# A fused expert, attention, expert block: GpSimd normalises half of the second layer's tokens early, and unread products and weight splits move

## The chip, the cores and the metric

The kernel runs on one core of a Trainium2 chip. The metric is the device time of one execution in microseconds; of the kernel before, three timed runs are given and their median is the time to be beaten. An expert stage, an attention stage and a second expert stage run one after the other in a single launch.

## What is computed

The input x has 8 sequences of 256 tokens with 256 features. The reference does three residual steps:

```python
x = x + 0.5 * ffn(layernorm(x), router_w, w1, v1, w2)   # "layer 0" of the kernel
x = x + attn(layernorm(x), Wq, bq, Wk, bk, Wv, bv, Wo, bo)
x = x + 0.5 * ffn(layernorm(x), router_w, w1, v1, w2)   # "layer 1" of the kernel
```

The expert step routes each of the 2048 tokens to 8 of 64 experts by the softmax of the router's logits, normalises the 8 weights, keeps the first 32 tokens of each expert, and computes `(silu(x w1) * (x v1)) w2` for these 64 x 32 slots, which are added back to their tokens by weight. Attention has 16 query heads and 4 key/value heads of 128, all in float32 accuracy.

## The kernel before, in words

**Tiling.** x stays on chip as 16 tiles of 128 tokens (`x`, 128 x 16 x 256). Experts are taken in 16 groups of 4, so that 4 experts x 32 slots fill 128 partitions. Attention runs in 4 blocks of 512 tokens with 16 steps each (2 heads of one sequence by a step).

**An expert stage** (`expert_layer` on each engine). TensorE transposes the tokens and makes the logits; VectorE finds the top 8 (`masks`, L875) and the keys of the first 32 tokens of each expert (L900 to L932, ending in `slot_token` and `slot_index`). Meanwhile ScalarE normalises the tokens into `xn` (`normalise`, L606), GpSimd makes the weights `expw` (L506 to L528), and SyncE writes both to `token_table` in HBM (`store_table`, L405). When `slot_index` is ready and all table writes have landed (`table_written`, L531), GpSimd gathers the slots, one indirect DMA for each group (L538), five in flight.

**The expert steps** (`slot_step`, 17 of them, s = 0 to 16). In step s TensorE transposes the slots of group s + 1 (L1179), adds up the results of group s - 3 (`sum_slots`: L1191 in layer 1 only, L1207), transposes the hidden values of group s - 1 (L1242), multiplies group s up (L1249) and group s - 1 down (L1259). ScalarE copies the transposed slots (L564) and hidden values (L568), makes the gate (L574) and the high half of y (L578); VectorE the weight of the slots (L851 to L855), the one-hot marks (L858), `hidden` (L864) and the low half of y (L871). A chain of dependences runs through a step: up, gate, hidden, transpose, copy, down. All queues are in order.

**Unread products.** `keep_busy` (L1211) multiplies `router_w` by `ident` into a bank that nobody reads. It stands where TensorE has nothing to do: 16 products before step 0, 20 after layer 0's steps, 12 more in layer 1's routing, 4 after the first transposes of attention.

**Splits.** The attention weights come as float32 and are split into two float32r parts: `split_high(n)` on ScalarE (L677), then `split_low(n)` on VectorE (L998). They go by number: 0 and 1 are Wk, 2 and 3 the first part of Wq, 4 and 5 Wv, 6 and 7 the next part of Wq, 8 and 9 Wo, 10 and 11 Wq, and so on. Splits 0 and 1 are done in the last two steps of layer 0, 2 to 5 after them; the others between the first 9 projections of attention (`first_fills`) and the steps of its first block.

**Order of loads.** SyncE's queue loads the experts' weights into places that are reused; layer 1's groups 0 to 6 are loaded from step 12 of the last attention block on (L446 to L449), groups 7 and 8 after the wait for `attention_done`, and behind them come layer 1's stores to the table. GpSimd's own queue waits for `attention_done` before it begins layer 1 (L546).

**Layer norms.** `moment_steps` (L802) makes mean and 1/std on VectorE in short linked instructions. For layer 1 those of tiles 0 to 11 are made in steps 11 and 12 of the last block; `shifts(0, 12)` (L1153), which frees ScalarE to normalise them, comes after its last step.

## Time and profile before

| | us |
|---|---|
| median of 3 timed runs | 658.8 (658.24 to 660.04) |
| the profiled execution | 656.91 |
| its span in the profile | 655.1 |
| layer 0, until the last sum of its steps | 0 to 84.4 |
| attention | about 85 to 567 |
| layer 1's routing, to `slot_index` | about 566 to 590.3 |
| layer 1's steps and output | 594.5 to 655.1 |

| engine | busy us | share of the span |
|---|---|---|
| PE (TensorE) | 617.7 | 94% |
| DVE (VectorE) | 502.9 | 77% |
| ACT (ScalarE) | 386.3 | 59% |
| POOL (GpSimd) | 52.0 | 8% |

How to read it: busy time is a mean over stages with different limits, and a busy PE isn't one at its peak. What a change in one stage is worth is read from that stage, from what its waits ended on. Rows of the timeline give start (us from the start of the span), duration (us), engine, line, operation, tiles, shapes and count, and in brackets the idle time of the engine before it and who ended it.

### The profile page before, as it was taken

Reading aid. Unit: us, or ns where it says so; the run is one execution under the profiler, and the core shown is the slowest. Engines: PE = TensorE matmul, PEld = TensorE weight load, DVE = VectorE, ACT = ScalarE, POOL = GpSimd, SP = SyncE. Lnnn points to the kernel's source line nnn. Section 1 sums busy time; section 2 is a strip of 40 time slices with the busy share of each in tenths; the row PEclk is TensorE's granted clock in tenths of the full one; section 3 lists DMA queues with packets and bytes.
Section 4 is the critical chain, followed back from the end, with each engine's and each line's share of the span. In section 5 each row is a group of like instructions: output and inputs, shape, how many; then the busy total and the mean of one; then the engine's idle time right before and its main releaser. Section 6 shows DMA issues by size and latency. Waiting matters only on the chain.

```text
span 655.1 us, 12187 instructions
## 1 busy us (share of the span) xinstructions
PE 617.7 (94%) x4572; PEld 533.3 (81%) x4572; DVE 502.9 (77%) x1316; ACT 386.3 (59%) x1048; POOL 52.0 (8%) x75
## 2 busy tenths in 40 slices
PE   7489989999999999999999999999999998987995
PEld 5367677999889989999889999989899997764774
DVE  6746668889988778889777788877788888693663
ACT  5734476677666655666665666656566665581442
POOL 3443000000000000000000000000000000034310
PEclk9699999999999999999999999999999999987999
DMA  8999760000000000000000000000000009476781
GB/s 315 352 417 420 295 257 1 2 1 1 1 2 1 1 2 1 1 1 2 1 2 1 2 0 1 2 2 1 1 1 2 1 11 419 172 265 220 293 310 43
DMA packets 27621, 62.53 MB, mean 95 GB/s; under 512 B 7014, under 2 KB 17382, under 8 KB 27558
## 3 DMA queue, kind: packets, MB, share of 16 engines
q1 hardware_dynamic: 25398, 55.97, 22.7%
q0 software_dynamic: 1664, 5.30, 2.2%
q8 instruction: 39, 0.64, 0.4%
q10 hardware_dynamic: 496, 0.43, 0.3%
q14 instruction: 24, 0.20, 0.1%
HBM read 54.34 MB, written 7.34 MB: 94 GB/s over the span
## 4 chain that ended last, share of the span: by engine, by line
PE 78%; DVE 10%; DMA 6%; ACT 2%; issue 1%; another core or an unknown queue 1%; POOL 0%; SPq 0%; POOLq 0%; DVEq 0%
PE bank L1407 20%; PE bank L1409 19%; PE bank L1408 19%; PE bank L1463 8%; PE bank L1207 4%; PE bank L1249 3%; DMA slots<-token_table,slot_index 2%; DMA wo_raw<-wo_in 2%; PE bank L1259 2%; PE bank L1179 1%; DVE probsT_lo L1107 1%; DMA x<-x_in 1%; DVE negmax L1072 1%; DVE ln L812 1%; DVE struck L891 1%
## 5 line engine op out<-in xcount | busy, mean ns | idle before, releaser
L724 ACT ACTIVATE probs<-bank,negmax 128x256 f32<-128x256 f32 x256 | 121.4, 494 | 0.7 <-DVE negmax L1072 0.6
L732 ACT CAST probsT_hi<-bank 128x512 fp32r<-128x512 f32 x128 | 68.7, 590 | 71.0 <-PE bank L1463 71.0
L707 ACT ACTIVATE o_hi<-bank,bv 128x512 fp32r<-128x512 f32 x64 | 44.2, 690 | 66.7 <-PE bank L1409 66.7
L1107 DVE TENSOR_TENSOR probsT_lo<-bank,probsT_hi 128x512 fp32r<-128x512 f32 x128 | 81.9, 681 | 0.5 <-ACT probsT_hi L732 0.5
L1072 DVE TENSOR_REDUCE negmax<-bank 128x2 f32<-128x512 f32 x128 | 81.8, 680 | 0.0
L1080 DVE TENSOR_SCALAR probs<-probs,rowinv 128x256 f32<-128x256 f32 x256 | 73.1, 349 | 2.3
L1407 PE MATMUL bank<-wo_hi,o_hi 128*128 128x256 f32 x256 | 73.1, 285 | 0.0
L1409 PE MATMUL bank<-wo_hi,o_lo 128*128 128x256 f32 x256 | 72.6, 284 | 0.0
L1408 PE MATMUL bank<-wo_lo,o_hi 128*128 128x256 f32 x256 | 72.3, 282 | 0.0
L1058 DVE SCALAR_TENSOR_TENSOR o_lo<-bank,bv,o_hi 128x512 fp32r<-128x512 f32 x64 | 48.0, 750 | 28.6 <-ACT o_hi L707 28.4
L1463 PE MATMUL bank<-ident,probs 128*128 128x128 f32 x512 | 66.4, 273 | 0.7 <-DVE probs L1080 0.7
L1463 PEld LDWEIGHTS bank<-ident,probs 128*128 128x128 f32 x512 | 57.3, 140 | 1.1 <-DVE probs L1080 1.1
L724 ACT ACTIVATION_READ_ACCUMULATOR probs<-bank,negmax 128x1 f32 x256 | 57.7, 226 | 0.0
L1407 PE MATMUL bank<-xT_hi,wq_hi 128*128 128x512 f32 x128 | 54.4, 425 | 1.0 <-DVE k_even_lo L1058 1.0
L1407 PE MATMUL bank<-probsT_hi,v_hi 128*128 128x512 f32 x128 | 51.1, 399 | 3.1 <-DVE probsT_lo L1107 2.9
L1409 PE MATMUL bank<-xT_hi,wq_lo 128*128 128x512 f32 x128 | 50.4, 394 | 0.0
L1408 PEld LDWEIGHTS bank<-wo_lo,o_hi 128*128 128x128 f32 x256 | 48.3, 189 | 2.5
L1407 PEld LDWEIGHTS bank<-wo_hi,o_hi 128*128 128x128 f32 x256 | 48.4, 189 | 2.3
L1408 PE MATMUL bank<-probsT_lo,v_hi 128*128 128x512 f32 x128 | 50.1, 392 | 0.0
L1408 PE MATMUL bank<-xT_lo,wq_hi 128*128 128x512 f32 x128 | 50.1, 392 | 0.0
L1409 PE MATMUL bank<-probsT_hi,v_lo 128*128 128x512 f32 x128 | 50.0, 391 | 0.0
L1409 PEld LDWEIGHTS bank<-wo_hi,o_lo 128*128 128x128 f32 x256 | 48.4, 189 | 0.0
(191 smaller groups left out, 1393.2 us busy)
## 6 DMA issues: line engine op xcount, KB each, us to landing
up_r_<-up_in SPq DMA_DIRECT2D x16, 768.0 KB
down_r_<-down_in SPq DMA_DIRECT2D x14, 512.0 KB
up_q<-up_in SPq DMA_DIRECT2D x8, 768.0 KB, 8.7
up_o<-up_in SPq DMA_DIRECT2D x6, 768.0 KB
down_q<-down_in SPq DMA_DIRECT2D x8, 512.0 KB, 9.4
token_table<-xn SPq DMA_DIRECT2D x16, 256.0 KB, 2.4
down_o<-down_in SPq DMA_DIRECT2D x6, 512.0 KB
x<-x_in SPq DMA_DIRECT2D x4, 512.0 KB, 5.6
```

What stands on the lines that cost most here:

```text
L707: nc.scalar.activation(dst, src, ACT.Identity, bias=bias).then_inc(work_high, 1)
L724: nc.scalar.activation(probs[:, n % 2, t, :], scores_ps[head][:, qt * S:qt * S + S], ACT.Exp, bias=negmax[:, n % 2, t:t + 1], accum_out=ro ...
L732: nc.scalar.copy(probsT[0][:, head].rearrange("p c s -> p (c s)"), probsT_ps[head][:]).then_inc(probsT_high, 1)
L1058: nc.vector.scalar_tensor_tensor(lo, src, bias, hi.bitcast(f32), ALU.add, ALU.subtract).then_inc(work_taken, 1)
L1072: nc.vector.reduce_max(negmax[:, n % 2, 2 * head:2 * head + 2], scores_ps[head][:].rearrange("p (t s) -> p t s", t=2), AX.X, negate=True). ...
L1080: last = nc.vector.tensor_scalar(probs[:, n % 2, t, :], probs[:, n % 2, t, :], rowinv[:, n % 2, t:t + 1], None, ALU.mult)
L1107: nc.vector.tensor_tensor(probsT[1][:, head].rearrange("p c s -> p (c s)"), probsT_ps[head][:], probsT[0][:, head].rearrange("p c s -> p ( ...
L1207: last = mm(banks[n][:, D * pair:D * pair + D], marks[:, c:c + P], parts, start=start and pair == 0, stop=stop, skip_group_check=True)
L1407: mm(dst, w[0], m[0], start=start, stop=False, skip_group_check=shared)
L1408: mm(dst, w[0], m[1], start=False, stop=False, skip_group_check=shared)
L1409: return mm(dst, w[1], m[0], start=False, stop=stop, skip_group_check=shared)
L1463: last = nc.tensor.transpose(probsT_ps[head][:, c * S + qt * P:c * S + qt * P + P], probs[:, n % 2, 2 * head + qt, c * P:c * P + P], ident[:])
```

## The change

1. **GpSimd normalises tiles 0 to 7 of layer 1** into a new buffer `early_xn`, which lies where `wv` was, as soon as `moments_ready` reaches 2; `shifts(0, 12)` moves from behind the last step to the end of step 12 of the last block. SyncE writes these rows to the table behind the loads of groups 0 to 6, ahead of its wait for `attention_done`. ScalarE normalises only tiles 8 to 15 in layer 1, 8 to 11 ahead of the two exponentials, 12 to 15 behind them, and the order of stores follows that.
2. **Unread products**: 4 at the head of step 0, 3 in step 1, 4 in step 2 of both layers (those of step 2 into bank 4, behind a wait for `limit_ready`); 14 instead of 20 after layer 0's steps.
3. **Step 16**: of the sums of group 13 only bank 6's stay ahead of the hidden transpose; bank 7's come behind it.
4. **Splits**: `split_high(0)` moves from the end of step 15 to step 16 behind the hidden copy, `split_high(1)` behind y; `split_low(1)` behind the steps; `split_high` 6 to 10 come after projections 1 to 5, 11 after the last one (before: 6 and 7 ahead of all, 8 to 11 after projections 1 to 4).

```diff
         wk = [sb(ctx, f"wk_{n}", [P, KD, KV * DH], f32r) for n in ("hi", "lo")]
+        with ExitStack() as lent:
+            early_xn = sb(lent, "early_xn", [P, TILES // 2, D])
         wv = [sb(ctx, f"wv_{n}", [P, KD, KV * DH], f32r) for n in ("hi", "lo")]
...
+            def store_early_tokens(n):
+                sp.wait_ge(early_ready, 4 * n + 4)
+                store_rows(n, early_xn)
...
             def store_table(layer):
-                store_tokens(0)
                 if layer == 0:
+                    store_tokens(0)
                     store_tokens(1)
-                store_weights(0)
+                    store_weights(0)
+                store_tokens(2)
                 if layer == 1:
-                    store_tokens(1)
-                    store_weights(1)
-                store_tokens(2)
-                if layer == 0:
-                    store_weights(1)
+                    store_weights(0)
+                store_weights(1)
                 store_tokens(3)
...
             for g in range(len(homes_q) + 3):
                 load(1, g)
+            for n in range(2):
+                store_early_tokens(n)
             sp.wait_ge(attention_done, 1)
...
             expert_layer(0)
+            pool.wait_ge(moments_ready, 2)
+            for a in range(TILES // 2):
+                nc.gpsimd.tensor_scalar(early_xn[:, a, :], x[:, a, :], mean[:, a:a + 1], rstd[:, a:a + 1],
+                                        ALU.subtract, ALU.mult).then_inc(early_ready, 1)
             pool.wait_ge(attention_done, 1)
...
                 if layer == 0 and s == GROUPS:
-                    split_high(1)
+                    split_high(0)
...
-                if layer == 0 and s == GROUPS - 1:
-                    split_high(0)
+                if layer == 0 and s == GROUPS:
+                    split_high(1)
...
-                stops = ((8, 8), (4, 6))[layer]
-                normalise(0, stops[0])
+                middle = (TILES // 2, TILES - 4)[layer]
+                normalise(TILES // 2 * layer, middle)
                 for h in range(2):
                     act.wait_ge(scaled_ready, 2 * layer + h + 1)
                     nc.scalar.activation(expw[:, 8 * h:8 * h + 8, :], expw[:, 8 * h:8 * h + 8, :], ACT.Exp).then_inc(exps, 1)
-                    if h == 0:
-                        normalise(*stops)
                 act.wait_ge(moments_ready, 2 * layer + 1)
-                normalise(stops[1], TILES)
+                normalise(middle, TILES)
...
-            for n in range(6, 8):
-                split_high(n)
             act.wait_ge(bq_scaled, 1)
             for n, job in enumerate(first_fills):
                 take_fill(*job)
-                if 1 <= n < 5:
-                    split_high(n + 7)
+                if 1 <= n < 6:
+                    split_high(n + 5)
+                if n == len(first_fills) - 1:
+                    split_high(11)
...
                 if layer == 0 and s == GROUPS:
                     split_low(0)
-                    split_low(1)
...
                 if layer == 0:
+                    split_low(1)
                     split_low(2)
...
+                if last and n == 12:
+                    shifts(0, TILES - 4)
...
-            shifts(0, TILES - 4)
             for t in range(2):
                 spread_of(BLOCKS - 1, t)
...
+                if s == 0:
+                    keep_busy(4)
                 if s < GROUPS:
                     pe.wait_ge(slotsT_ready, sT_seen.add())
                 if s + 1 < GROUPS:
                     transpose_slots(s + 1, (s + 1) % RING)
-                if s >= 3:
+                if s == GROUPS:
+                    sum_slots(layer, s - 3, [0])
+                elif s >= 3:
                     sum_slots(layer, s - 3)
+                elif s == 2:
+                    pe.wait_ge(limit_ready, layer + 1)
+                    keep_busy(4, bank[4])
+                elif s == 1:
+                    keep_busy(3)
                 if s > 0:
                     pe.wait_ge(hidden_ready, hidden_seen.add())
                     nc.tensor.transpose(bank[2][0:F, 0:P], hidden[:],
                                         ident[:]).then_inc(hiddenT_raw, 1)
+                if s == GROUPS:
+                    sum_slots(layer, s - 3, [1])
...
                 if layer == 0:
-                    keep_busy(20)
+                    keep_busy(14)
```

## Rows read from the trace of the kernel before

**Rows 1.** The page: the chain that ended last, by engine.
```profile
PE 78%; DVE 10%; DMA 6%; ACT 2%; issue 1%; another core or an unknown queue 1%; POOL 0%; SPq 0%; POOLq 0%; DVEq 0%
```
**Rows 2.** The chain in order of time (start, us, what), around layer 1's step 0.
```profile
596.62 3.31 another core or an unknown queue
```
**Rows 3.** Windows: us, busy PE, PEld, DVE, ACT, POOL, then PEclk, DMA share, GB/s.
```profile
593.70:600.50 6.80, 2.26 (x24) 1.10 (x23) 1.51 (x7) 1.26 (x4) 3.89 (x5) 0.85 0.50 138
600.50:605.50 5.00, 4.95 (x48) 2.54 (x52) 3.18 (x14) 1.52 (x5) 0.95 (x1) 0.52 1.02 408
```
**Rows 4.** Timeline, layer 0's steps 1 and 5: when hidden was ready, what TensorE waited for.
```profile
40.78 0.25 DVE L864 TENSOR_TENSOR hidden<-gate,bank 128x96 f32<-128x96 f32 x1 [2.02 <-ACT gate L574]
...
41.20 0.27 PE L1242 MATMUL bank<-ident,hidden 128*96 128x128 f32 x1
...
50.16 0.41 PE L1179 MATMUL bank<-ident,slots 128*128 128x128 f32 x2 [0.27 <-DMA slots<-token_table,slot_index]
```
**Rows 5.** Timeline, layer 0's step 16, TensorE and ScalarE.
```profile
80.10 0.27 PE L1242 MATMUL bank<-ident,hidden 128*96 128x128 f32 x1
80.50 0.63 ACT L681 ACTIVATE wk_hi<-wk_raw 128x512 fp32r<-128x512 f32 x1 [0.75 <-DMA wk_raw<-wk_in]
81.03 0.24 ACT L568 COPY hiddenT<-bank 96x128 f32<-96x128 f32 x1
...
81.33 0.64 PE L1259 MATMUL bank<-down_r_,hiddenT 96*32 96x256 f32 x8 [0.96 <-ACT hiddenT L568]
```
**Rows 6.** Timeline, from the last sums of layer 0 to attention's first operand.
```profile
84.26 4.62 PE L1215 MATMUL bank<-router_w,ident 128*128 128x128 f32 x40
...
87.38 1.38 DVE L1046 TENSOR_SCALAR xn<-x,ln 128x256 f32<-128x256 f32 x4
...
89.19 1.13 ACT L681 ACTIVATE wq_hi<-wq_raw 128x512 fp32r<-128x512 f32 x2
...
90.54 1.07 ACT L705 CAST xT_hi<-bank 128x512 fp32r<-128x512 f32 x2 [0.22 <-PE bank L1430]
```
**Rows 7.** Timeline of ScalarE, the first projections.
```profile
93.92 0.63 ACT L681 ACTIVATE wo_hi<-wo_raw 128x512 fp32r<-128x512 f32 x1 [2.30 <-DMA wo_raw<-wo_in]
```
**Rows 8.** Timeline, the end of layer 1's routing: stores, indices, first gather.
```profile
586.34 2.58 SPq L396 DMA_DIRECT2D token_table<-xn  x4
...
590.11 0.17 DVE L932 TENSOR_SCALAR slot_index<-bank 128x16 uint32<-128x16 f32 x1
...
591.52 0.99 POOL L538 DMA_INDIRECT slots<-token_table,slot_index  x1 [7.11 <-issue]
```
**Rows 9.** Timeline of layer 0: the first gather behind its index (ready at 31.57).
```profile
31.87 1.07 POOL L538 DMA_INDIRECT slots<-token_table,slot_index  x1 [6.72 <-DVE slot_index L932]
```
**Rows 10.** Timeline of TensorE, layer 1: the up products of step 1 and of step 3.
```profile
600.93 1.51 PE L1249 MATMUL bank<-up_q,slotsT 128*32 128x192 f32 x16
...
607.52 0.86 PE L1249 MATMUL bank<-up_q,slotsT 128*32 128x192 f32 x16
```
**Rows 11.** Timeline, layer 1's step 16: hidden, and the down products.
```profile
643.11 0.26 DVE L864 TENSOR_TENSOR hidden<-gate,bank 128x96 f32<-128x96 f32 x1 [0.27 <-ACT gate L574]
...
644.99 0.64 PE L1259 MATMUL bank<-down_r_,hiddenT 96*32 96x256 f32 x8 [0.35 <-ACT hiddenT L568]
```
**Rows 12.** The chain in order of time, steps 12 and 14 of the last block.
```profile
550.52 0.17 DVE ln L812
...
559.85 1.15 DVE probs L1080 x4
```
**Rows 13.** Timeline, step 13 of the last block.
```profile
553.56 1.14 DVE L1080 TENSOR_SCALAR probs<-probs,rowinv 128x256 f32<-128x256 f32 x4
...
556.07 1.04 PE L1463 MATMUL bank<-ident,probs 128*128 128x128 f32 x8
```
**Rows 14.** Timeline of GpSimd in layer 1: a one-input copy, and two two-input products.
```profile
570.71 0.40 POOL L511 CAST key_of_group<-key_i 128x256 f32<-128x256 int32 x1
...
581.85 2.56 POOL L527 TENSOR_TENSOR expw<-expw,chosen 128x512 f32<-128x512 f32 x2
```

More of the change, by code:

```diff
@@ L233, in macaron_kernel @@
         xn_ready = sem("xn_ready")
+        early_ready = sem("early_ready")
         xnT_raw = sem("xnT_raw")
@@ L391, in _, with store_rows @@
             rows_of_table = table[0:T, :].rearrange("(h p b) e -> h p b e", h=2, p=P)
+            def store_rows(n, rows):
+                for half in range(2):
+                    sp.dma_start(rows_of_table[half, :, 2 * n:2 * n + 2, 0:D],
+                                 rows[:, 4 * n + half:4 * n + half + 3:2, :]).then_inc(table_written, 16)
             def store_tokens(n):
                 sp.wait_ge(xn_ready, xn_seen.add(4))
-                for half in range(2):
-                    sp.dma_start(rows_of_table[half, :, 2 * n:2 * n + 2, 0:D],
-                                 xn[:, 4 * n + half:4 * n + half + 3:2, :]).then_inc(table_written, 16)
+                store_rows(n, xn)
+            def store_early_tokens(n):
+                sp.wait_ge(early_ready, 4 * n + 4)
+                store_rows(n, early_xn)
             def store_weights(m):
@@ L1181, in transpose_slots, with sum_slots @@
                 last.then_inc(slotsT_raw, 1)
-            def sum_slots(layer, s):
+            def sum_slots(layer, s, banks=range(2)):
                 pe.wait_ge(marked, GROUPS * layer + s + 1)
@@ L1188, in sum_slots @@
                 marks = onehot[:, s % MARKS, :]
-                if layer == 1:
+                if layer == 1 and 0 in banks:
                     for low in range(2):
@@ L1194, in sum_slots @@
                         last.then_inc(bank_summed, 1)
-                for n in range(2):
+                for n in banks:
                     for low in range(2):
@@ L1199, in sum_slots @@
                         last.then_inc(bank_summed, 1)
-                if not final:
+                if not final and 1 in banks:
                     last.then_inc(summed, 1)
@@ L1209, in sum_wide, with keep_busy @@
                 return last
-            def keep_busy(count):
+            def keep_busy(count, unread=bank[3]):
                 for _ in range(count):
-                    mm(bank[3][:, 0:KD * E], ident[:], router_w[:].rearrange("p k e -> p (k e)"),
+                    mm(unread[:, 0:KD * E], ident[:], router_w[:].rearrange("p k e -> p (k e)"),
                        start=True, stop=True)
```

## The prediction

> **What bounds the kernel now.** I read the page first: the chain that ended last is TensorE for 78% and VectorE for 10% [rows 1]. In the 460 us of attention it is TensorE's queue almost throughout; the change touches that stretch only at its two ends, so it can gain or lose only there and in the two expert stages. So the second view is the chain in order of time at these places, and the third the timeline there. They show six spots. (1) In layer 0's first steps TensorE follows a dependence: hidden is ready at 41.03 and its transpose starts at 41.20 [rows 4]. (2) In step 16 of layer 0 ScalarE makes a split of Wk at 80.50, so the hidden copy comes at 81.03 though the transpose began at 80.10, and the down products start at 81.33 [rows 5]. (3) At the start of attention TensorE is held by 20 unread products and ScalarE by two splits of Wq, until xT at 90.54 [rows 6]; then ScalarE, whose queue has a split of Wo next, waits 2.30 us for the load of Wo that lands at 93.9 [rows 7], while a finished k product sits in its bank. (4) Layer 1's indices are ready at 590.28, but the first gather starts at 591.52, because the last four stores to the table were issued from 586.34 to 588.92 [rows 8]. (5) Right behind it the chain has 3.31 us of "another core or an unknown queue" on ScalarE ahead of its first gate [rows 2], and TensorE, busy 2.26 of 6.80 us, falls to a granted clock of 0.52, its lower level, for the next 5 us [rows 3]. (6) In layer 1's step 16 hidden is ready at 643.37 and the down products start at 644.99 [rows 11], eight to ten sums in between.
>
> **The change part by part.** The sum is made against the profiled execution, 656.91 us with a span of 655.1; the median of the runs shown is 658.8, 1.9 above it, and I carry differences over.
>
> *Unread products in layer 0.* One product costs 4.62 / 20 = 0.23 us at full clock [rows 6]. The four of step 0 fall into a wait for the second gather and cost nothing. The three of step 1 and four of step 2 stand ahead of a hidden transpose whose operand is ready by then (0.17 us earlier in step 1 [rows 4]), so all of them go onto the path: 7 x 0.23 = 1.6. Step 5 waited 0.27 us for its gather [rows 4]; that wait goes. Together +1.3 (bounds 0, if the waits on ScalarE's copies swallow more than I see, and +1.6). Their added wait for `limit_ready` is idle: VectorE makes it at 41.4, ahead of step 2. The weights' loads aren't late through this, they are a backlog of the DMA queues until 76 us.
>
> *Step 16 of layer 0.* From the start of the transpose to down 80.10 to 81.33 = 1.23 us. Without the split in front the copy of 0.24 follows the transpose of 0.27, so down comes about 0.6 after it: -0.6. And the transpose itself no longer waits for all eight sums (1.2 us as a group), but for four: -0.6. So -1.2, and the last sum ends about where it did, at 84.4 + 0.1.
>
> *From there to xT.* `split_low(1)` now stands with `split_low(2)` ahead of the layer norm's statistics: one VectorE split of 0.69 less what was waiting, +0.45 on the tokens' normalisation, which ends at 88.76 [rows 6], so 89.2. TensorE has 6 x 0.23 = 1.4 us less in front of the token transposes, so it is waiting for the tokens rather than the other way. ScalarE's two splits of 1.13 us [rows 6] are out of the way. xT comes at about 89.65 instead of 90.54: -0.9.
>
> *The wait for Wo.* The k product then ends near 92.7 and ScalarE, with Wq's split next instead of Wo's, takes it at once: k at 92.7 instead of 94.45, -1.8 in all. Wo's first split now comes after the third projection behind xT, at about 94.5, when Wo (93.9, not moved) has landed. The splits of 0.6 each that are pushed back, 10 and 11, land on ScalarE when it waits for TensorE anyhow, but 11 stands ahead of the first copies of step 0; I give 0.3 for it. **Attention starts 1.5 us earlier** (bounds -2.0, everything kept, and -0.3, if the 0.9 at xT fails and the splits take back the rest).
>
> *The last block.* `shifts(0, 12)` goes from an idle place into step 12, where the chain goes through the linked layer-norm instructions: the last before the maxima is 0.17 us [rows 12], so one more is +0.2. GpSimd starts its eight instructions then, at 550.9. No row shows its tensor_scalar; a one-input copy of 256 elements takes 0.40, and a two-input product of 512 elements 2.56 / 2 = 1.28 [rows 14]. I take 0.5, nearer to the copy, as there is one tensor input: 8 x 0.5 = 4 us, ended at 555. The four stores (1 MB) go into a SyncE queue that then waits until 570, behind seven groups' loads. Cost 0 (bounds: -0.1; the upper one is the rival below).
>
> *Layer 1's table.* ScalarE's eight instructions and four of eight token stores leave. The last store is issued at about 586.4 instead of 588.9; by the 2.6 us that lay between the last issue and the gather [rows 8] it is free at 589.0, ahead of the indices at 590.28. In layer 0 the gather starts 0.3 us behind its index [rows 9]; so 590.56, 0.96 earlier. But the 16 unread products end at 593.7, and the four new ones of step 0 delay the second transposes a little: I count -0.6 (bounds -0.9 and 0).
>
> *Layer 1's first steps.* If the 3.31 us on ScalarE stay, the three products of step 1 lie under them; the four of step 2 cost +0.9. In return TensorE is busy some 1.6 us more before 599, and I take it that the clock stays at its upper level. The price of the lower one: the up products took 1.51 instead of 0.86 [rows 10], and the whole of steps 1 and 2 about 5.3 us against 3.3 in layer 0: -2.0 (bounds -2.3; and +0.5, if the clock falls all the same and the four products cost 0.36 each).
>
> *Layer 1's step 16.* Down 1.6 us behind hidden [rows 11]; with four sums behind the transpose it is 0.5 less. -0.5 (bounds -0.6 and -0.2).
>
> **Sum:** +1.3 - 1.2 for layer 0, -1.6 for the rest up to attention's first steps (together -1.5), +0.2, -0.6, +0.9 - 2.0, -0.5 = **-3.5**, so 653.4 against 656.9 profiled, and 658.8 - 3.5 = **655.3** for the median.
>
> **The rivals.** (A) *ScalarE's 3.3 us go away.* Its queue is 8 instructions shorter there, and at 596.7 an instruction packet crosses the DMA engines, just as the wait begins; in all other steps none such is seen. If it hangs on the place in the instruction stream, it may vanish: step 1 then waits for the third gather and its products, so another 1.6 us: -5.1, 653.7. Against it: other such packets stall nobody. By the Trainium skill (Runtime: NRT & Kernel Launch, Instruction fetch mechanics) an engine fetches the next block of instructions while it executes the present one, mostly hidden; that would speak for another cause, and this trace doesn't settle it. (B) *The clock falls all the same, or the wait moves into a later step.* Then the first steps are +0.5 instead of -1.1, in all -1.9: 656.9. (C) *Slower: GpSimd blocks VectorE in the last block.* In step 13 four probability scalings of 1.14 us run at 553.56, with 1.4 us of slack to the transpose at 556.07 [rows 13]; those at 559.85 are on the chain [rows 12]. If each of them waited for one GpSimd instruction of 1.28 us, the first four cost 5.1 - 1.4 = 3.7 and the next, as GpSimd isn't done by then, some 2.5: -3.5 + 6.2 = +2.7, 661.5. It decides from about 1.0 us an instruction; at 0.5 the slack takes nearly all. For it: nothing else in the trace of attention runs on GpSimd, so it is untried there. Against it: GpSimd's products in the routing run beside VectorE's work whose durations don't change. The Trainium skill has a rule that speaks against the change here (SBUF — State Buffer, Who interferes with whom): VectorE's tensor_scalar in its two-port mode and GpSimd share a port pair, and the later one blocks fully until the first is done. By it each of the first four would wait for up to one instruction, which at 0.5 us is 2.0 less the slack, +0.6 on the sum. No row of before shows such a pair. (D) *The start of attention gives nothing*, as VectorE's splits, which are as many as before, set its pace: -3.5 + 1.8 = -1.7, 657.1.
>
> **How the numbers follow.** Forecast 0.40, A 0.22, B 0.18, C 0.07, D 0.13. The measurement can tell about 0.3%, 2.0 us, from no change. Faster by more than that: the forecast, A, and a third of B and D (by their bounds), 0.72; within: 0.22; slower: 0.06. The forecast's own bounds of the front (-0.3 to -2.0) give 654.8 to 656.5; A reaches below it to 652.9, B and D above it to 658.2. The range is 652.8 to 658.2; left out are C and the corners.
>
> **What would show it.** Steps 1 to 3 of layer 0 later by 0.7 and 1.6 us, its last sum at 84.4 +- 0.3; xT below 90; no wait of ScalarE for Wo, and the first scores 1.5 us earlier; GpSimd's eight instructions from 551 on and their duration, VectorE's scalings beside them still 1.14 for four; first gather of layer 1 0.3 us behind `slot_index`; PEclk 1.00 from 593 on; and the 3.3 us on ScalarE in the same place or not. The forecast is wrong if the clock falls there, if GpSimd's instructions take over 1 us, or if attention's first steps don't keep the lead.

## The result, and the profile after

| | before | after |
|---|---|---|
| median of 7 timed runs each, same chip, us | 658.8 (658.03 to 661.45) | 655.21 (653.68 to 657.38) |
| ratio, 95% interval | | 0.9949 [0.9932, 0.9966] |
| profiled execution, its span | 656.91, 655.1 | 656.69, 654.6 |

The kernel after is 0.5% faster: 658.8 x 0.0051 = 3.4 us, between 2.2 and 4.5. The forecast was 655.3, 3.5 less. But the two profiled executions differ by 0.2 us only, so one pair of traces can't explain the medians: that of before lies below all its timed runs, and that of after is among the slower of its own. The reading needs the stages, and more than one profile of each kernel.

**Start of attention, in after** (answers to [rows 6, 7]). The timeline of TensorE, then of ScalarE, then windows (us, busy time of PE, PEld, DVE, ACT, POOL, then PEclk, DMA share, GB/s):

```profile
84.89 3.29 PE L1228 MATMUL bank<-router_w,ident 128*128 128x128 f32 x28
90.38 1.09 PE L1454 MATMUL bank<-ident,xn 128*128 128x128 f32 x8 [2.21 <-DVE xn L1058]
```
```profile
91.13 1.07 ACT L717 CAST xT_hi<-bank 128x512 fp32r<-128x512 f32 x2 [1.45 <-PE bank L1454]
92.09 0.64 ACT L693 ACTIVATE wq_hi<-wq_raw 128x512 fp32r<-128x512 f32 x1
95.39 0.69 ACT L719 ACTIVATE k_even_hi<-bank,bk 128x512 fp32r<-128x512 f32 x1 [2.66 <-PE bank L1433]
```
```profile
91.00:92.00 1.00, 1.00 (x10) 1.00 (x9) 0.25 (x1) 0.87 (x2) 0.00 (x0) 0.78 1.09 389
92.00:95.00 3.00, 3.00 (x11) 2.52 (x11) 1.63 (x3) 0.73 (x2) 0.00 (x0) 0.50 0.40 140
95.00:96.00 1.00, 1.00 (x6) 0.81 (x5) 0.00 (x0) 0.61 (x2) 0.00 (x0) 1.00 0.00 0
```

The wait for Wo is gone, as forecast. The products end at 84.89 + 3.29 = 88.2, 0.7 us earlier than in before. But TensorE takes up the tokens at 90.38, 2.2 us later, although the first of the four normalised pieces was there at about 88.7. Behind this idle time the clock stands at 0.50, its lower level, for 3 us, and k is taken at 95.39 instead of 94.45: in this execution the front gave nothing.

**The last block, in after** (answers to [rows 12 to 14]), GpSimd and VectorE:

```profile
552.10 9.81 POOL L558 TENSOR_SCALAR early_xn<-x,ln 128x256 f32<-128x256 f32 x8 [483.46 <-DVE ln L854]
```
```profile
551.82 0.18 DVE L854 SCALAR_TENSOR_TENSOR ln<-ln 128x12 f32<-128x12 f32 x1
...
554.86 1.31 DVE L1092 TENSOR_SCALAR probs<-probs,rowinv 128x256 f32<-128x256 f32 x4
...
561.17 1.41 DVE L1092 TENSOR_SCALAR probs<-probs,rowinv 128x256 f32<-128x256 f32 x4
```

GpSimd's instruction takes 9.81 / 8 = 1.23 us, not 0.5. The scalings beside it take 1.31 and 1.41 us for four instead of 1.14.

**Layer 1, in after** (answers to [rows 2, 3, 8, 11]): index and first gather; the chain at step 0; the clock; step 16.

```profile
592.12 1.04 POOL L548 DMA_INDIRECT slots<-token_table,slot_index  x1 [6.19 <-DVE slot_index L943]
```
```profile
598.30 2.57 another core or an unknown queue
```
```profile
598.00:600.00 2.00, 1.08 (x8) 0.92 (x8) 0.00 (x0) 0.30 (x1) 1.13 (x2) 1.00 0.51 145
600.00:602.00 2.00, 0.52 (x9) 0.37 (x13) 0.76 (x5) 0.68 (x3) 0.00 (x0) 1.00 0.86 310
602.00:604.00 2.00, 2.00 (x33) 1.49 (x26) 1.47 (x6) 1.08 (x4) 0.68 (x1) 1.00 0.99 374
```
```profile
643.59 0.27 PE L1264 MATMUL bank<-ident,hidden 128*96 128x128 f32 x1
643.62 0.71 PE L1220 MATMUL bank<-y_parts,onehot 128*128 128x256 f32 x4
644.26 0.64 PE L1283 MATMUL bank<-down_r_,hiddenT 96*32 96x256 f32 x8
```

The gather starts 0.44 us behind the start of `slot_index` (591.68), in before 1.41 [rows 8]. The unknown wait ahead of the first gate is still there; this time the clock holds behind it.

### The profile page after: what moved, and what is told of

It is laid out like the page before. It is cut to its first block, busy times and chain, and to the rows that moved or that the text cites. A ratio compares the mean times of both kernels' runs of the same rounds, so it can differ in the third digit from the quotient of the medians.

```text
span 654.6 us, 12253 instructions
## 1 busy us (share of the span) xinstructions
PE 622.7 (95%) x4604; PEld 539.4 (82%) x4604; DVE 503.5 (77%) x1316; ACT 382.4 (58%) x1040; POOL 61.7 (9%) x83
## 4 chain that ended last, share of the span: by engine, by line
PE 83%; DVE 11%; ACT 2%; DMA 2%; issue 1%; another core or an unknown queue 0%; POOL 0%; POOLq 0%; SPq 0%; DVEq 0%; ACTq 0%
PE bank L1431 20%; PE bank L1433 19%; PE bank L1432 19%; PE bank L1487 8%; PE bank L1220 4%; PE bank L1273 4%; PE bank L1283 2%; PE bank L1192 2%; PE bank L1228 1%; DVE ln L824 1%; DVE probsT_lo L1119 1%; DVE negmax L1084 1%; DMA slots<-token_table,slot_index 1%; DVE struck L902 1%; PE bank L1299 1%
## 5 line engine op out<-in xcount | busy, mean ns | idle before, releaser
L558 POOL TENSOR_SCALAR early_xn<-x,ln 128x256 f32<-128x256 f32 x8 | 9.8, 1235 | 483.5 <-DVE ln L854 483.5
```

## The experiments

The first four kernels ran on one chip (A), the last eight on another (B). The kernel before, timed beside them, took 655.66 us on A, 658.83 and 659.04 on B. Which chip the first pair of profiles ran on isn't on record; before took 658.8 there. Ratios are to before on the same chip, and differences in us with an interval are worked out from the ratio. Below, "the statistics" are the first of the layer norm's instructions behind layer 0, `BATCH_NORM_STATS2` on VectorE.

**1. The early normalisation alone.** Before, plus part 1 of the change: the lines of the diff with `early_xn`, `store_table`, `shifts` and ScalarE's `normalise`.

> Only the first part of the change on the kernel before: GpSimd's eight normalisations, SyncE's early stores, ScalarE's shorter list and the new order of the table's stores; expert steps and splits as before. If its price is what the profile of after shows (0.2 us for the two shifts in step 12, some 0.4 us for the probability scalings beside GpSimd) and its gain is the first gather 1.0 us earlier, it is -0.4 us against before, and TensorE's granted clock in layer 1's steps 1 and 2 still falls to about 0.52. If GpSimd's work costs the last block more than those two groups show (its eight instructions took 9.8 us instead of the 4 forecast), it is +0.5 to +2 us and the sums of the last block end that much later. If the shorter list of ScalarE also ends its 3.3 us wait, -2.5 us or more.

Measured: 654.77 us, 0.9988 [0.9972, 1.0004], so -0.8 +- 1.0 us. The gather starts 0.44 us behind the index here too. What wasn't expected: the long wait isn't there, and TensorE's clock holds without a single product in the steps. Timeline of ScalarE, then a window:

```profile
597.75 0.25 ACT L588 ACTIVATE gate<-bank 128x96 f32<-128x96 f32 x1 [0.45 <-PE bank L1262]
```
```profile
601.00:605.00 4.00, 4.00 (x62) 2.75 (x61) 3.39 (x13) 1.85 (x8) 1.06 (x2) 1.00 1.01 407
```

**2. The unread products alone.**

```diff
+                if s == 0:
+                    keep_busy(4)
...
+                elif s == 2:
+                    pe.wait_ge(limit_ready, layer + 1)
+                    keep_busy(4, bank[4])
+                elif s == 1:
+                    keep_busy(3)
```

> Only the eleven unread products in each layer's steps 0 to 2, on the kernel before. By the forecast's terms: +1.3 us in layer 0 and -1.1 us in layer 1 (+0.9 for the four of step 2, -2.0 because the clock stays at its upper level), so +0.2 us in all. Rival: the clock needs the earlier gather too and falls all the same in layer 1: +2.5 us. Second rival: layer 0's products hide in waits there: -1 us. Marks: start of the transposes of layer 0's step 3 (before 44.53), granted clock of layer 1's steps 1 and 2 (before 0.52).

Measured: 657.47 us, 1.0025 [1.0009, 1.0042]: 1.6 us slower on this chip. From the first gathered slots to the hidden transpose of step 5, layer 1 takes 15.58 us against 14.34 and 14.17 in experiments 1 and 3: the products cost 1.3 us, and there is no fall of the clock to save, as the long wait is missing. The clock was 1.00 through the steps of both layers, so the first rival (a fall all the same) isn't it.

**3. The splits, and 14 products behind layer 0, alone.** The cut diff leaves out the moves of `split_high(0)`, `split_high(1)` and `split_low(1)`, which are in the kernel too.

```diff
-            for n in range(6, 8):
-                split_high(n)
...
-                if 1 <= n < 5:
-                    split_high(n + 7)
+                if 1 <= n < 6:
+                    split_high(n + 5)
+                if n == len(first_fills) - 1:
+                    split_high(11)
...
-                    keep_busy(20)
+                    keep_busy(14)
```

> Only the moved splits of Wk, Wq and Wo and 14 instead of 20 unread products after layer 0, on the kernel before. The forecast's theory (the products and ScalarE's two splits of Wq hold xT back): xT about 0.9 us earlier than 90.54, k 1.8 us earlier, in all -2 us or better. The theory formed from the profile of after (TensorE's next instructions come in 2.6 us behind its q8 packet whatever the number of products; six products fewer only leave it idle, and the clock falls): xT where it was, 90.5 +- 0.3, the wait for Wo gone, the granted clock at 92 to 95 us down to 0.5 in the profile or in some of the executions, in all between -1.2 and +0.3 us.

Measured: 653.50 us, 0.9955 [0.9939, 0.9971], so -3.0 +- 1.0 us. In time and in k the forecast's theory holds, and the one formed from the profile of after falls. One part of the latter stays: TensorE takes up the tokens at 90.12, after 1.61 us of idleness and 2.4 us behind an instruction packet (87.75). ScalarE's timeline:

```profile
90.87 1.08 ACT L705 CAST xT_hi<-bank 128x512 fp32r<-128x512 f32 x2 [0.45 <-PE bank L1430]
91.83 0.64 ACT L681 ACTIVATE wq_hi<-wq_raw 128x512 fp32r<-128x512 f32 x1
93.91 0.69 ACT L707 ACTIVATE k_even_hi<-bank,bk 128x512 fp32r<-128x512 f32 x1 [1.44 <-PE bank L1409]
```

Counted from the layer norm's statistics (85.34), k is taken 8.57 us later; in experiments 1 and 2, with the old splits, 10.28 and 10.38.

**4. After with 20 products behind layer 0** (`keep_busy(14)` to `keep_busy(20)`).

> The kernel after with 20 instead of 14 unread products after layer 0. If TensorE's resumption behind the branch hangs on the number of products, as the forecast had it, xT comes up to 1.4 us later than in after (91.13) and the kernel is 0.5 to 1.4 us slower than after (655.2), about 656.2. If it hangs on the fetch of its instructions, xT stays at 91.1 +- 0.2, the clock stays at 1.00 through 91 to 95 us, k is taken about 0.9 us earlier, and the kernel is 0.5 to 1.5 us faster than after: about 654.2.

Measured: 652.52 us, 0.9947 [0.9928, 0.9966]; after itself has 0.9949. xT is at 90.40, 5.21 us behind the statistics, in after 6.13. So neither sentence fits: six products more cost nothing in this execution, and the late resumption isn't a constant either. Between this kernel and experiment 2 nothing differs at the front but the splits, both with 20 products: k is taken 8.28 and 10.38 us behind the statistics. In both, TensorE resumes without an idle stretch, and there the splits make the whole gain. Where it resumes late they don't: see experiment 8.

**5. After again, on chip B.**

> The kernel after itself, on the chip of this call, as the basis for the next three. In the profiles of before and after the 3.3 us (2.6 us) wait stands ahead of layer 1's first gate; in the four kernels measured since, on one other chip, it does not. If it belongs to the program's instruction stream, it is here again in this kernel (one with 12 more TensorE instructions had none); if it belongs to the chip or to the single execution, it may be missing. Against before the ratio should be 0.995 as measured, if the wait is in neither; about the same if it is in both.

Measured: 655.77 us, 0.9953 [0.9934, 0.9972]. The long wait is back (2.57 us), in a kernel that is word for word that of the first profile; and the front now looks quite different from it. TensorE and ScalarE:

```profile
85.66 3.29 PE L1228 MATMUL bank<-router_w,ident 128*128 128x128 f32 x28
89.55 1.74 PE L1454 MATMUL bank<-ident,xn 128*128 128x128 f32 x8 [0.60 <-DVE xn L1058]
```
```profile
90.94 1.07 ACT L717 CAST xT_hi<-bank 128x512 fp32r<-128x512 f32 x2
...
94.01 0.69 ACT L719 ACTIVATE k_even_hi<-bank,bk 128x512 fp32r<-128x512 f32 x1 [1.47 <-PE bank L1433]
```
```profile
92.00:95.00 3.00, 2.88 (x14) 2.17 (x12) 1.71 (x4) 1.53 (x4) 0.00 (x0) 1.00 0.82 286
```

TensorE goes on as soon as the first piece of the tokens is there (VectorE makes them from 89.08), the clock stays at 1.00, and k comes 8.24 us behind the statistics (85.77).

**6. After without layer 1's products in steps 0 to 2** (the three conditions get `layer == 0 and`).

> After without the eleven unread products of layer 1's steps 0 to 2. The forecast's term: they are worth -1.1 us (the clock at its upper level against 0.9 us of products), so without them +1.1 us, and the granted clock falls to about 0.5 in steps 1 and 2. The theory from the last four profiles: the clock falls only behind the 3.3 us wait; where that is missing the clock stays at 1.00 without any product, and the products are a pure price of 0.7 us up to the first hidden transpose and 0.7 us in steps 1 and 2. So without them -1.4 us against after where the wait is missing, about +1 where it is there.

Measured: 655.68 us, 0.9949 [0.9924, 0.9974], the same as experiment 5. In the profile the forecast's mechanism is plain to see, with the wait of 3.48 us and the clock behind it:

```profile
598.58 0.25 ACT L588 ACTIVATE gate<-bank 128x96 f32<-128x96 f32 x1 [3.48 <-remote]
```
```profile
601.00:605.00 4.00, 4.00 (x40) 1.54 (x32) 2.13 (x8) 1.51 (x5) 1.38 (x2) 0.50 1.02 421
```

From the first slots to step 5 it takes 19.16 us against 17.42. Why 1.7 us in the profile are nothing in the medians is seen in experiment 8.

**7. Six more products in layer 0, where TensorE is idle** (`keep_busy(6)` behind layer 0's `take_tokens()`), and **both edits of 6 and 7 together**.

> After with six more unread products in layer 0, at a place where TensorE stands idle for 4.7 us (behind the tokens' products, ahead of the slot keys); 14 remain at layer 0's end. By the count of products behind layer 0, as the forecast had it, nothing changes: xT at 91.1 as in after, 655.2. By the position theory (the block of instructions that TensorE needs behind its branch is fetched 1.5 to 2 us earlier when the branch stands at least eleven products further on in its stream: packet at 85.6 instead of 87.7 us, as in the two kernels with 11 more products than before) TensorE goes on at 89.5 or earlier, xT comes at 90.4 +- 0.2, bound by ScalarE's table load, the clock stays at 1.00, k is taken 1.5 to 2 us earlier than in after: -1.5 us.

> Both edits together: six more products ahead of layer 0's slot keys, none in layer 1's steps. By my theory the two are independent: -1.5 - 1.4 = -2.9 us against after where the long wait is missing. By the forecast's terms 0 + 1.1.

Measured: 655.13 us, 0.9946 [0.9926, 0.9965], and 655.42 us, 0.9954 [0.9936, 0.9973]: both as after. k comes 8.29 and 8.33 us behind the statistics, as in experiment 5, so there was nothing left to gain in an execution of that form; -1.5 us was a comparison with the first profile.

**8. After without layer 0's products in steps 0 to 2**, and **after without any in either layer and 20 behind layer 0.**

> After without the eleven unread products in layer 0's steps 0 to 2; those of layer 1 stay. The forecast gave them +1.3 us: without them -1.3 us against after, so a ratio to before of 0.993. My theory now, that they hide in waits for the gathers and for ScalarE: at most -0.4 us, ratio 0.9945, with 14.6 +- 0.3 us from the first slots to the hidden transpose of step 5 in the profile, as in after (14.87 and 14.63).

> After without any unread product in the steps of either layer and with 20 instead of 14 behind layer 0. On a chip where the long wait ahead of layer 1's first gate is missing, the products are a pure price: 1.4 us or more faster than after, ratio to before 0.992 or better, clock at 1.00 throughout layer 1. On a chip with that wait the clock falls behind it to 0.5 for some 6 us, and the time is that of after within 1.5 us, by the profiles rather above it: ratio 0.995 to 0.998.

Measured: 656.77 us, 0.9968 [0.9951, 0.9985], and 656.74 us, 0.9964 [0.9950, 0.9978]. Neither is faster than after (0.9953). Layer 0's eleven products are no price of 1.3 us, and the trace of the first shows why: without them the clock falls there. Windows, then TensorE:

```profile
41.00:44.00 3.00, 3.00 (x36) 1.52 (x32) 1.65 (x8) 0.88 (x3) 0.00 (x0) 0.56 1.02 422
...
601.00:605.00 4.00, 4.00 (x33) 2.70 (x32) 2.25 (x10) 1.33 (x4) 0.94 (x1) 0.50 1.02 406
```
```profile
40.33 1.51 PE L1273 MATMUL bank<-up_q,slotsT 128*32 128x192 f32 x16
```

The up products take 1.51 instead of 0.86 us. And the second window is layer 1, where this kernel has its products: the clock fell all the same.

At the start of attention these two kernels differ in nothing but 14 and 20 products behind layer 0, and in both profiles TensorE resumes late with the clock at 1.00 behind it. ScalarE in the second kernel (20), counted from its statistics at 85.90:

```profile
92.31 1.07 ACT L717 CAST xT_hi<-bank 128x512 fp32r<-128x512 f32 x2 [1.21 <-PE bank L1447]
93.27 0.64 ACT L693 ACTIVATE wq_hi<-wq_raw 128x512 fp32r<-128x512 f32 x1
95.38 0.69 ACT L719 ACTIVATE k_even_hi<-bank,bk 128x512 fp32r<-128x512 f32 x1 [1.47 <-PE bank L1426]
```

xT comes 6.41 us behind them and k 9.48, with the splits out of the way; with 14 products it is 5.82 and 8.89. Between these two profiles six products are a price of 0.6 us.

**9. GpSimd's eight instructions done twice.**

```diff
+            for a in range(TILES // 2):
+                nc.gpsimd.tensor_scalar(early_xn[:, a, :], x[:, a, :], mean[:, a:a + 1], rstd[:, a:a + 1],
+                                        ALU.subtract, ALU.mult).then_inc(early_twice, 1)
+            pool.wait_ge(early_twice, 8)
```

> After with GpSimd's eight normalisations done twice, one batch behind the other, so some 19.7 us of GpSimd work in the last block, to 571.5 us. The second batch lies beside two more groups of VectorE's work. If GpSimd only slows VectorE's instructions beside it, as the four scalings show (1.14 us without it, 1.27 to 1.42 beside it), nothing moves by more than 0.3 us, ratio to before as after, 0.995, or 0.9955. If each VectorE instruction beside it had to wait for the end of one of GpSimd's (the rival of the forecast), ten or more instructions behind 562 would be 1 us later each: over 5 us slower.

Measured: 656.65 us, 0.9966 [0.9948, 0.9984]. GpSimd and VectorE:

```profile
549.90 9.81 POOL L559 TENSOR_SCALAR early_xn<-x,ln 128x256 f32<-128x256 f32 x8 [481.63 <-DVE ln L859]
559.81 9.74 POOL L563 TENSOR_SCALAR early_xn<-x,ln 128x256 f32<-128x256 f32 x8
```
```profile
558.97 1.64 DVE L1097 TENSOR_SCALAR probs<-probs,rowinv 128x256 f32<-128x256 f32 x4
...
570.04 0.68 DVE L1111 TENSOR_TENSOR x<-x,bank 128x512 f32<-128x512 f32 x1
```

From step 13's scalings (552.65) to the last addition (570.04) it is 17.39 us, in experiment 5 16.99 (553.47 to 570.46), in before 16.87 (553.56 to 570.43): GpSimd's eight instructions cost 0.1, and eight more 0.4. The five microseconds of the blocking rival are far off. In this profile, too, the clock fell in layer 1 in spite of the products.

**10. Before again, on chip B**, a profile and one time.

> The kernel before itself, for a profile on the chip of this call, since the first profile of before had a layer 0 that was 1.4 us shorter, from its first slots to the hidden transpose of step 5 (13.83 us), than any profile since, the two of kernels without products in layer 0's steps among them (14.72 and 14.74). If that stretch is set by the gathers, it is here 14.6 +- 0.3 us; by the forecast's reading, in which the products of after cost 1.3 us, it is 13.8 and the two others were slow for another cause.

Measured: 658.39 us. The stretch is 13.85 us, as in the first profile of before, with the clock up (the window that fell to 0.56 in experiment 8):

```profile
41.00:44.00 3.00, 2.94 (x43) 1.64 (x43) 1.99 (x10) 1.68 (x6) 0.44 (x1) 1.00 1.03 425
```

So the gathers don't set it, and my expectation fails. The forecast's reading half holds: experiments 1 and 3, which took 14.7 us without any product, weren't slow for an unrelated cause; their clock fell in the same place.

## Why the prediction was right

The time was right to 0.1 us, but not each term, so part of that closeness is luck: errors of either sign cancelled. The best pair to read it from is that of one chip, experiments 10 and 5. Stage by stage, in us:

| from the event above to | before | after | difference | forecast |
|---|---|---|---|---|
| first gathered slots of layer 0 | 38.05 | 39.09 | +1.04 | 0 |
| hidden transpose of step 5 | 13.85 | 14.63 | +0.78 | +1.3 |
| layer norm's statistics | 32.93 | 32.05 | -0.88 | -1.2 + 0.45 |
| k taken by ScalarE | 10.45 | 8.24 | -2.21 | -2.25 |
| last maxima of attention | 462.40 | 462.71 | +0.31 | +0.3 + 0.2 |
| first gathered slots of layer 1 | 37.71 | 36.93 | -0.78 | -0.6 |
| hidden transpose of step 5 | 18.76 | 17.42 | -1.34 | +0.9 - 2.0 |
| last sum | 35.23 | 34.83 | -0.40 | -0.5 |
| end | 7.21 | 7.29 | +0.08 | 0 |

The first row isn't the kernels' doing: it lies between 37.5 and 39.2 in the 12 profiles in which no edit touches it (39.6 and 38.8 in experiment 7, which has six more products there), and the last one, untouched in all 14, between 5.6 and 7.9. In the first pair of profiles they made +0.7, the stages between them -1.2 instead of -4.5, above all because k was taken 10.39 us behind the statistics instead of 8.24: that is why those two executions could be 0.2 apart.

The clock is the other reason. Over the 14 profiles:

| stretch | kernels | profiles with the clock at 0.5 there | us from the first slots to step 5 |
|---|---|---|---|
| layer 0, no products in the steps | before (2), exp. 1, 3, 8 (2) | 4 of 6 | 13.8 without, 14.7 to 15.0 with |
| layer 0, eleven products | the other 8 | 0 of 8 | 13.9 to 14.9 |
| layer 1 with the long wait, no products | before (2), exp. 6, 7 (second), 8 (second) | 5 of 5 | 18.5 to 19.4 |
| layer 1 with the wait, products | after (2), exp. 7 (first), 8 (first), 9 | 2 of 5 | 17.4 to 17.6 without, 20.3 with |
| layer 1 without the wait (chip A) | exp. 1 to 4 | 0 of 4 | 14.2 and 14.3 without products, 15.6 and 15.7 with |

The third place is layer 1's routing, where the clock is at 0.5 in all 14 profiles, for 3.4 us in seven and for 6.8 us in the other seven.

Point by point:

*Layer 0's products and step 16, +1.3 and -1.2.* The products are mis-sized: +0.8 up to step 5 where the clock holds without them. And they keep it up in stretches where it would have fallen in four of six profiles, at 0.9 to 1.2 us each by step 5, which the forecast hadn't seen as before showed none. But neither amount reaches the stage's end in full, because the two terms aren't independent. In before, ScalarE's split of Wk waits 0.75 us for its load [rows 5], 1.00 in experiment 10; in experiment 1, with the same step 16 but everything 0.9 us later because of the clock, the load has landed and it waits for nothing:

```profile
81.38 0.63 ACT L693 ACTIVATE wk_hi<-wk_raw 128x512 fp32r<-128x512 f32 x1
82.09 0.26 ACT L582 COPY hiddenT<-bank 96x128 f32<-96x128 f32 x1
```

So the down products come 2.0 and 2.3 us behind hidden in the two profiles of before, 1.4 in experiment 1, 1.1 in every kernel with the whole change. From the first slots to the statistics it is 46.5 and 46.8 us in before, 46.7 in experiment 1, 46.7 in experiment 5: the forecast had +0.55 for this stretch, and the best pair has -0.1. The step 16 term is right in size there only because the split was also waiting for a load, which the forecast didn't name. In the medians the products cost nothing that can be measured.

*The front.* Right in size: k was to come 1.8 us earlier with statistics 0.45 later, so -2.25 from these, and it is -2.21. Of this, xT makes 1.37 (6.53 us behind the statistics in experiment 10, 5.16 in 5; forecast 0.9 + 0.45) and the wait for Wo that is gone 0.85 (k 3.92 and 3.07 behind xT; forecast 0.9). The forecast named two things that hold xT back, ScalarE's splits and TensorE's 20 products. Both do, though on TensorE's side it is products and a late resumption together. With the old splits and no idle stretch on TensorE (experiment 2) xT comes at 6.27; with the new splits and 20 products but a late resumption (experiment 8, second) at 6.41; with the new splits and a late resumption behind 14 products at 5.53, 5.82 and 5.49 (experiments 3, 8 and 9); with the new splits and no late resumption at 5.16 to 5.27, whether 14 products (experiments 5 to 7) or 20 (experiment 4). Either holder alone keeps nearly all of the delay. Rival D is out.

*The clock and TensorE's branch.* Behind layer 0's steps stands a test on a register, the `If` of the late tokens, which is jumped over. In each of the 14 profiles the view of the DMA queues, in stretches of 0.1 us, has an instruction packet of queue q8 near it (taken for TensorE's, as its packets move when products are added to TensorE's stream: 85.8 in experiment 2, 87.3 in before), at one of two moments: in eight of them 2.2 to 3.3 us behind the start of the statistics, and then TensorE takes up the tokens 2.4 to 2.5 us after the packet (in after: packet 87.9, tokens 90.38); in six no more than 1.0 us behind it, and then nothing waits. Of the six profiles without products in layer 0's steps all have it late; of the four with 14 behind layer 0 and eleven in the steps two (after and experiment 9 against 5 and 6); of the four with six more products than that none. So it goes with how far on in TensorE's stream the branch stands, with one place in between where it goes either way. The experiment that was to show this as the cause, 7, can't, as after itself had the early packet on that chip. The Trainium skill (Runtime: NRT & Kernel Launch, Instruction fetch mechanics) has a rule for such a place: a taken branch whose target isn't among the two blocks held makes the engine wait until that block is fetched by DMA. The traces agree with it, with 2.4 to 2.5 us from the packet to the first matmul; which block a packet carries they don't show. What it costs where the clock holds depends on the products ahead of it: k at 8.56 to 8.89 us behind the statistics with 14 (experiments 3, 8 first and 9), 9.48 with 20 (8 second), against 8.22 to 8.33 without it; where the clock falls behind it, as in after, all of the front's gain.

*The last block.* +0.31 for `shifts` and what attention's first steps give back. GpSimd's price per instruction was the term with the largest error, 1.23 us instead of 0.5: it passed the 1.0 us from which I had rival C decide. C still didn't come, as its other half was wrong: no VectorE instruction waits through a whole one of GpSimd's. The four scalings beside GpSimd grow from 1.14 us to 1.26 to 1.43, in experiment 9 once to 1.64. The growth isn't spread over the four: in experiment 5 one of them takes 0.49 us instead of 0.35, and it lies across the moment at which one of GpSimd's instructions ends and the next begins (554.03 to 554.52, the border at 554.37); the longest, in the first of experiment 8, takes 0.64. The Trainium skill (SBUF — State Buffer, Who interferes with whom) has it that beside a VectorE instruction in its two-port mode the later one fully blocks; no trace here shows a wait of 1.2 us, and whether these scalings use that mode isn't seen in one.

*Layer 1's table, -0.6.* Right: -0.78, by the gather that starts 0.44 instead of 1.41 us behind the index. That compares like with like, a clock fall of 3.4 us in the routing in both. With the early normalisation the row is 36.9 to 37.1 us in the five profiles with the short fall and 37.3 to 37.8 in the five with the long one, so the length of that fall, which the forecast didn't have, is worth as much as the term. Both profiles of before and both of after have the short one; whether the kernel or the execution sets it stays open.

*Layer 1's first steps, -1.1.* Right in the execution where the clock holds (-1.34), but rival B is as real: in two of five profiles with the wait it falls in spite of the products, and then the stretch takes 0.9 to 1.8 us more than without them. A mean of (3 x 17.5 + 2 x 20.3) / 5 = 18.6 against 18.9 for the five without fits the medians of experiments 5 and 6, which show no difference. On chip A the same products are a price of 1.3 us. So the ratio hardly depends on this term, but the reason for it in the forecast, "the clock stays", is true only sometimes.

*Layer 1's step 16, -0.5.* Right: -0.40, and the down products come 1.22 instead of 1.63 us behind hidden.

*The 3.3 us wait (rival A).* It seems not to be the program's. It stood in all ten profiles on chip B and on that of the first pair (2.6 to 3.5 us), in none of four on chip A, under instruction streams that differ little; before itself is 3.2 to 3.4 us faster on A, though no kernel was profiled on both chips. The instruction packet that the forecast saw beside it (596.4 in before) doesn't make it by itself: one of the same queue stands between 594.9 and 598.3 in all 14 profiles, the four without the wait among them. In before TensorE's up products are recorded from 596.14 for 0.86 us, and their semaphore rises at 599.93, together with those of the two transposes behind them: so it isn't ScalarE's queue, on which the profile books the wait. What holds TensorE there is open.

*The sum.* All stages but the first and the last make -4.52 in this pair (forecast -3.4 by the table), the timed runs -3.1 (experiment 5) and -3.4 by their ratios. Experiment 5's profile is the favourable form at every place: TensorE resumes early, the clock holds in layer 1's steps, and its fall in the routing is the short one. The difference is of the size of two falls of the clock in layer 1's steps in five executions, 0.4 x 2.8 = 1.1 us. That the timed runs fall as often as the profiles is assumed, not shown. So the total was right because several gains were a little larger than forecast and layer 0's price smaller, and because a risk that I had kept for a rival was at work in part of the executions.

## What to carry to other kernels

Where a single trace is set against another, cut both at the same events and see which stages repeat in a second trace before a term is believed: here two stages that no edit touches scattered over 1.6 and 2.3 us, and the granted clock of a short stretch differed between executions of one and the same program. Unread products to hold the clock are an insurance: eleven of them cost 1.3 us in layer 1 on the chip where the engine wasn't waiting, so put them where it waits in every execution, and look for the fall in several profiles. Of two things that seem to hold the same operand, take each away alone and both together, in each form that the executions take: here either ScalarE's splits or TensorE's late resumption alone kept nearly all of xT's delay, and the gain came only with both gone. And a gain of 0.9 us in the middle of a stage isn't one at its end while a later step still waits for a load.

## What the runs showed of the hardware

- TensorE resumed 2.4 to 2.5 us after an instruction packet behind a branch in eight profiles, and without any wait in six whose packet came earlier; the same program did both.
- One `tensor_scalar` of GpSimd with two scalars from a tile takes 1.23 us for 128 x 256 floats, VectorE's on the same shape (`xn` [rows 6]) 1.38 / 4 = 0.35. Beside it, four VectorE scalings of 1.14 us in all took 1.26 to 1.64, the growth in one or two of them.
- A wait of 2.6 to 3.5 us on TensorE's completions stands in the same place in all ten profiles of chip B and of the first pair, and in none of the four on chip A; before is 3.2 to 3.4 us faster on A.
- In layer 1's routing the granted clock is at its lower level for 3.4 us in seven profiles and for 6.8 us in seven. With the early normalisation the stage is 0.6 us longer with the longer fall, by the means of five profiles each.
